# Three rotating score banks, maxima by halves, and nine-column turning products in a two-layer decoder kernel

## The reference, cut to what matters

```
h  = layernorm(x);  x = x + Wo . attention(q, k, v of h, 16 heads of 8, causal, q and k normalised per head) + bo
h  = layernorm(x);  x = x + Wproj . attention(h; ctx, 16 heads of 8, window |i-j| <= 64) + bproj
h  = layernorm(x);  x = x + mxfp4_quantised(h) . mxfp4_quantised(W) + bias
attention = softmax over the keys of (q.k + mask), times v
```

## Time and profile before

| what | us |
|---|---|
| median of three runs | 1455.29 |
| the profiled execution | 1459.37 |
| its span | 1457.6 |
| span from the first maximum of the third phase to the end | 516.3 |
| PE busy in it, DVE, ACT, POOL | 452.04, 354.21, 317.53, 320.32 |

### The profile page before, as it was taken

How to read it: one execution, slowest core, us unless ns; L and a number is a source line. 1 busy time by engine, 2 the same in 40 slices (tenths; PEclk the granted TensorE clock), 3 DMA queues, 4 the chain that set the end, 5 groups by cost and what they waited for, 6 DMA issues and landing times.

```text
span 1457.6 us, 42538 instructions
## 1 busy us (share of the span) xinstructions
PE 1294.8 (89%) x15257; PEld 942.1 (65%) x15257; DVE 1081.9 (74%) x2573; ACT 1049.3 (72%) x2841; POOL 633.9 (43%) x844
## 2 busy tenths in 40 slices
PE   4358999999999999999984999889889989999995
PEld 1125676666666666767674999856656666676664
DVE  6998889999899988876665344466668778686665
ACT  2128999999999999999981566647666766766653
POOL 0012424353444434310215554448675776655663
PEclk9999999999999999999995999979999999999997
DMA  6942242413214241020112332220101010000000
GB/s 145 242 121 57 52 102 53 113 49 95 66 48 100 52 108 49 16 94 2 52 35 66 101 96 75 96 84 22 32 10 42 11 41 11 26 25 4 25 11 16
DMA packets 83579, 89.00 MB, mean 61 GB/s; under 512 B 15792, under 2 KB 72752, under 8 KB 78768
## 3 DMA queue, kind: packets, MB, share of 16 engines
q1 hardware_dynamic: 77424, 77.10, 20.3%
q0 software_dynamic: 4096, 8.40, 2.0%
q10 hardware_dynamic: 1856, 0.79, 0.2%
HBM read 64.76 MB, written 17.83 MB: 57 GB/s over the span
## 4 chain that ended last, share of the span: by engine, by line
PE 60%; DVE 13%; ACT 10%; issue 8%; POOL 5%; DMA 2%; ACTq 0%; another core or an unknown queue 0%; DVEq 0%; SPq 0%; POOLq 0%
PE P L796 7%; PE P L958 7%; PE P L2114 5%; PE P L1579 4%; PE P L1612 4%; PE P L814 3%; PE P L940 3%; ACT pr L1019 3%; PE P L917 3%; PE P L928 3%; PE P L912 3%; PE P L2176 2%; PE P L2132 2%; PE P L835 2%; PE P L2069 2%
## 5 line engine op out<-in xcount | busy, mean ns | idle before, releaser
L2433 DVE TENSOR_REDUCE mx<-P 128x8 f32<-128x1024 f32 x128 | 156.5, 1223 | 123.8 <-PE P L2114 85.3
L1019 ACT ACTIVATE pr<-P,nm 128x256 f32<-128x256 f32 x512 | 238.6, 499 | 5.9 <-DVE nm L1217 5.7
L2326 ACT ACTIVATE et<-P 128x1024 f32<-128x1024 f32 x128 | 131.0, 1024 | 122.6 <-PE P L2121 110.2
L1217 DVE TENSOR_REDUCE nm<-P 128x4 f32<-128x1024 f32 x128 | 156.1, 1219 | 25.9 <-PE P L796 23.5
L796 PE MATMUL P<-kt_w,qt 64*128 64x256 f32 x1024 | 145.2, 402 | 4.6 <-ACT pr L1019 4.6
L1001 ACT COPY ptS<-P 128x512 f32<-128x512 f32 x256 | 138.1, 598 | 8.7 <-PE P L814 8.4
L992 ACT ACTIVATE pr<-pr,ri 128x256 f32<-128x256 f32 x254 | 119.6, 536 | 24.6 <-DVE pr L1190 24.0
L704 POOL TENSOR_TENSOR kv_qk<-kv_qk,mixing 128x512 f32<-128x512 f32 x48 | 61.0, 1271 | 151.9 <-DVE pr L1190 151.9
L1675 ACT ACTIVATE hT<-P,mixing 128x128 f32<-128x128 f32 x284 | 81.0, 368 | 61.1 <-PE P L1579 56.8
L698 POOL TENSOR_TENSOR kv_qk<-kv_qk,r_w 128x512 f32<-128x512 f32 x48 | 61.0, 1270 | 145.6 <-DVE pr L1190 100.0
L1019 ACT ACTIVATION_READ_ACCUMULATOR pr<-P,nm 128x1 f32 x512 | 118.2, 231 | 0.0
(11 more groups left out here) (351 smaller groups left out, 3652.4 us busy)
## 6 DMA issues: line engine op xcount, KB each, us to landing
kv_qk<-scr_v SPq DMA_DIRECT2D x16, 1024.0 KB, 8.0
r_w<-scr_r SPq DMA_DIRECT2D x16, 1024.0 KB, 10.8
xt<-scr_xs SPq DMA_DIRECT2D x71, 64.0 KB, 1.8
scr_ys<-yt SPq DMA_DIRECT2D x71, 64.0 KB
x<-in_x SPq DMA_DIRECT2D x8, 256.0 KB, 10.2
scr_v<-mixing SPq DMA_DIRECT2D x8, 256.0 KB, 2.5
scr_r<-mixing SPq DMA_DIRECT2D x8, 256.0 KB, 2.0
xb<-in_x SPq DMA_DIRECT2D x8, 256.0 KB, 3.3
```

The lines of the kernel that those rows point to most:

```text
L1019: e = nc.scalar.activation(pr[:, s % 3, h * KEYS:(h + 1) * KEYS], scores(s)[:, h // 2, (h % 2) * KEYS:(h % 2 + 1) * KEYS], ACT.Exp, bias=n ...
L1217: nc.vector.tensor_reduce(nm[:, s % 3, 0:4].rearrange("p (a h) -> p a h", a=2), scores(s).rearrange("p a (h k) -> p a h k", k=KEYS), AX.X, ...
L2326: nc.scalar.activation(et[:, u % 4, :, :, :], scoresT, ACT.Exp).then_inc(S["h_exp"], 1)
L2433: nc.vector.tensor_reduce(mx[:, n % 2, 8 * r:8 * r + 8].rearrange("p (k a) -> p k a", k=2), scores, AX.X, ALU.max, negate=True).then_inc(S ...
```

## The change

1. **Score banks.** Unit `s` puts its two halves of scores into banks `SCORE_BANKS[(2s+k) % 3]` of 0, 1 and 6. The mask of half `h` waits for the maximum of half `h-3` only. Each maximum is taken by halves, two instructions of 512 columns.
2. **Turning back** is done by two ordinary products with `ot` as weights and 36 columns of the identity (nine of each head's 32) instead of two transposes of 128 columns. The result has 144 columns and lies in bank 4 beside the output product.
3. **The output product** moves ahead of the turning back in PE's order, and its addition on DVE from the end of the slot to right behind the division.
4. **Projections** to q and k go in pairs (`qk0`, `qk1`: two products of 256 columns, one copy of 512 by ACT) through bank 7; their slots and some in `MIDDLE` change.
5. **The maxima** are turned between the masks and the scores of the next even slot, not at the odd slot's end.

```diff
-        "dxt": -25, "bias": -25, "qk0": -24, "qk1": -23, "qk2": -22, "qk3": -21, "square": -21, "v": -19, "reduce": -20,
+        "dxt": -25, "bias": -25, "qk0": -23, "qk1": -21, "square": -21, "v": -19, "reduce": -20,
...
-        "dxt": 11, "bias": 11, "qk0": 12, "qk1": 13, "qk2": 14, "qk3": 15, "square": 15, "v": 13, "reduce": 16,
+        "dxt": 11, "bias": 11, "qk0": 13, "qk1": 15, "square": 15, "v": 17, "reduce": 16,
...
-MIDDLE = (("qt0", 1), ("kt3", 1), ("qt3", 1), ("kt1", 2), ("kt2", 2), ("qt0", 3), ("kt1", 3), ("kt3", 3), ("qt2", 3),
+MIDDLE = (("qk0", 1), ("kt3", 2), *[(_name, _g) for _name in ("kt2", "qt1") for _g in range(4, GROUPS - 1)], ("qt0", 1), ("kt3", 1), ("qt3", 1), ("kt1", 2), ("kt2", 2), ("qt0", 3), ("kt1", 3), ("kt3", 3), ("qt2", 3),
...
+            SCORE_BANKS = (0, 1, 6)
-            qk_bank = P[:, 4, 2 * T:4 * T]
-            turned = P[:, 6, :]
+            turned = P[:, 4, T:T + H * (DH + 1)]
+            def score_bank(s, k):
+                return P[:, SCORE_BANKS[(2 * s + k) % 3], :]
+            def half(s, k):
+                return 2 * s + k + 1
...
+                def products(s, middle):
+                    for k in range(2):
+                        g = self_at(s, f"qk{k}")
+                        if g and ((f"qk{k}", g) in MIDDLE) == middle:
+                            bank7_free(f"qk{k}", g)
+                            pe.wait_ge(S["h7_read"], filled("dxt", g))
+                            for i in range(2):
+                                b = 2 * k + i
+                                m = nc.tensor.matmul(bank7[:, 256 * i:256 * i + 256], xTd[:, b * T:(b + 1) * T], wD[:, 0:256],
+                                                     start=True, stop=True)
+                            m.then_inc(S["h7"], 1)
...
-                        if s:
-                            pe.wait_ge(S["h_max"], s)
+                        if s == 0:
...
                         for k in range(2):
-                            nc.tensor.matmul(P[:, k, :], identb[:, :], bcast(maskb[:, local, :], 1, 4),
+                            if half(s, k) == 3:
+                                pe.wait_ge(S["m_y"], TILES)
+                            if half(s, k) > 3:
+                                pe.wait_ge(S["h_max"], half(s, k) - 3)
+                            nc.tensor.matmul(score_bank(s, k), identb[:, :], bcast(maskb[:, local, :], 1, 4),
                                              start=True, stop=False)
...
+                    if s % 2 == 0:
+                        maxima(s // 2 - 1)
                     for a in range(4):
...
-                        if qk_before[s + 1]:
-                            pe.wait_ge(S["qk_read"], qk_before[s + 1])
...
-                            m = nc.tensor.transpose(turned.rearrange("p (t a r x) -> p t r a x", t=2, a=2, r=2)[:, t, u % 2],
-                                                    ot[:, u % 2, t, :], ident[:, :])
+                            m = nc.tensor.matmul(turned.rearrange("p (t a r j x) -> p t r a j x", t=2, a=2, r=2, j=2)[:, t, u % 2],
+                                                 ot[:, u % 2, t, :],
+                                                 ident[:, :].rearrange("p (a j x) -> p a j x", a=2, j=2)[:, :, :, 0:DH + 1],
+                                                 start=True, stop=True)
...
-                    if s % 2:
-                        maxima(s // 2)
...
-                        nc.vector.tensor_reduce(mx[:, n % 2, 8 * r:8 * r + 8].rearrange("p (k a) -> p k a", k=2), scores,
-                                                AX.X, ALU.max, negate=True).then_inc(S["h_max"], 1)
+                        for k in range(2):
+                            nc.vector.tensor_reduce(mx[:, n % 2, 8 * r + 4 * k:8 * r + 4 * k + 4],
+                                                    score_bank(s, k).rearrange("p (a n) -> p a n", a=4),
+                                                    AX.X, ALU.max, negate=True).then_inc(S["h_max"], 1)
```

More of the change, by code:

```diff
@@ L2113, in score @@
                         cols, part = slice(b * T, (b + 1) * T), slice(64 * r + 32 * k, 64 * r + 32 * k + 32)
-                        return nc.tensor.matmul(scores[:, k, a, :], q[part, a, cols], keys[part, a, cols], start=False,
+                        return nc.tensor.matmul(score_bank(u, k)[:, a * T:(a + 1) * T], q[part, a, cols], keys[part, a, cols], start=False,
                                                 stop=(a == 3))
@@ L2155, in tensor_program @@
                                 m.then_inc(S["h_st"], 1)
+                    products(s, True)
                     operands(s, True)
@@ L2179, in tensor_program @@
                         m.then_inc(S["h_pv"], 1)
[L2182 to L2191, removed]
+                    u = s - 8
+                    if 0 <= u < UNITS_H and u % 2:
+                        n = pass_of(u)
+                        pe.wait_ge(S["h_oth"], n + 1)
+                        if n:
+                            pe.wait_ge(S["h_add"], n)
+                        if u + 1 < UNITS_H:
+                            pe.wait_ge(S["h_on"], n + 1)
+                        nc.tensor.matmul(wo_bank, oTh[:, n % 2, :], (wE if unit(u)[0] else wDo)[:, :], start=True,
+                                         stop=True).then_inc(S["h_wo"], 1)
                     u = s - 6
@@ L2214, in tensor_program @@
                         nc.tensor.transpose(oT_bank, on3[:, n % 2, :], ident[:, :]).then_inc(S["h_tr"], 1)
[L2215 to L2218, removed]
-                        if qk_before[s + 1]:
-                            pe.wait_ge(S["qk_read"], qk_before[s + 1])
[L2221 to L2235, removed]
+                    products(s, False)
                     g = self_at(s, "v")
@@ L2300, in operands, with products @@
                                                  scale=gbs[:, 6:7]).then_inc(S["h7_read"], 1)
+                def products(s, middle):
+                    for k in range(2):
+                        g = self_at(s, f"qk{k}")
+                        if g and ((f"qk{k}", g) in MIDDLE) == middle:
+                            got(f"qk{k}", g)
+                            if k == 0:
+                                act.wait_ge(S["d_qkn"], 2 * (g - 1))
+                            nc.scalar.copy(qkv[:, g % 2, 2 * k:2 * k + 2, :].rearrange("p b n -> p (b n)"), bank7)\
+                              .then_inc(S["h7_read"], 1)
                 for s in range(FIRST_H, LAST_H):
@@ L2344, in scalar_program @@
                           .then_inc(S["h_ot"], 1)
[L2346 to L2352, removed]
-                    turned_rows(s, False)
[L2355 to L2360, removed]
-                          .then_inc(S["p_qp_read"], 1)
+                    turned_rows(s, False)
+                    products(s, False)
                     g = self_at(s, "v")
@@ L2446, in vector_program @@
                                                 bcast(ri3[:, :], 2, DH), ALU.mult).then_inc(S["h_on"], 1)
+                    u = s - 8
+                    if 0 <= u < UNITS_H and u % 2:
+                        local, g, b, r = unit(u)
+                        n = pass_of(u)
+                        dve.wait_ge(S["h_wo"], n + 1)
+                        if local:
+                            dve.wait_ge(S["e_xb"], GS * g + b + 1)
+                        else:
+                            dve.wait_ge(S["d_xb"], g + 1)
+                        nc.vector.tensor_tensor(home(g)[:, b, :], home(g)[:, b, :], wo_bank, ALU.add)\
+                          .then_inc(S["h_add"], 1)
+                        dve.wait_ge(S["h_add"], n + 1)
                     g = self_at(s, "reduce")
```

48 lines of the change are left out of this document (13 added, 35 removed), and 4 rows, old and new, of tables (SELF, SELF_BY_SLOT).

## The result

The changed kernel takes 1462.04 us (median of 7 runs, 1459.03 to 1463.13) where the kernel before takes 1455.29 (7 runs): a ratio of 1.0041, interval 1.0029 to 1.0053. It is slower by 0.4%, where 1450 us, a gain, had been forecast. It is the outcome and the size of rival 1.

A forecast was written before the change was run, and what follows sets the result against it. PE was taken as the bound, busy 452 of 516 us in the third phase, with the scores-maximum-masks loop setting light slots. Terms -20 - 5 + 21 - 1 = -5 us gave about 1450 us, range 1437 to 1465 (8 in 10).

The forecast's parts named there:

- rival 1: Weight loads win: full slots pay 0.20 us, waits give 12, projections 3, turning back costs 25; 1465 us, chance 0.25.
- I take -20 us: PE's waits at masks and maxima product, 18.8 us listed: most go by rotation and moved maxima; ends -12 and -28.
- light slots shorter by 0.3 and full ones longer by 0.13: Third-phase slots: without bank-7 work 2.8 and 3.05 us, with four transposes 3.2 and 3.45.
- Together -5 us: Output product's wait for ACT's projection copy goes, projections pair: -6, +1.5, +1.6, -2; ends 0 and -9.
- +0.20 us a unit: Turning back on PE: four weight loads, 0.47 us against 0.27 until the next product; +25.6 us over 128 units.
- 4 us of cover: Part of the turning back's +25.6 us hidden where PE waits for POOL or late ACT, leaving +21 us.
- +10 to +29: Ends given for the turning back's net cost, taken as +21 us.
- The rest, -1: DVE's earlier addition, output product's wait for `on`, later maxima to ACT, earlier first masks: -1 us in all.
- point of decision: rival 1 decides once less than about 16 us of waits are recovered at a price of 21.
- Rival 4: Short products are cheap: turning back free or a gain of some 0.1 us a unit; 1416 us, chance 0.03.
- Rival 3: Longer slots give ACT, POOL, DVE time; PE's POOL waits shrink, cover 12 rather than 4; 1440 us, chance 0.16.

The follow-up runs named there:

- e9: The kernel before with the maxima moved and taken by halves, each mask waiting for its own bank's half, projections one by one; 1447.56 us.
- e4: The kernel before with paired projections, maxima moved and by halves, two score banks, old transposes, output product and addition as before; 1449.05 us.
- e5: The changed kernel with two score banks in place of three, each mask waiting for its own bank's last half; 1462.78 us.
- e7: The changed kernel with the turning back issued twice a unit, writing the same values; 1505.25 us.
- e10: The kernel before with the maxima by halves alone, the maxima product staying at the odd slot's end; 1450.22 us.
- e3: The kernel before with only the maxima moved, between masks and scores of the next even slot; 1454.22 us.
- e1: The kernel before with the nine-column turning back alone, in bank 6 as before; 1466.15 us.
- e2: The kernel before with only the projections in pairs through bank 7, with their tables; 1456.27 us.
- e8: The changed kernel with the output product behind the turning back, DVE's division waiting for it as well; 1463.89 us.
- e12: e11 with DVE's addition also moved right behind the division; 1448.12 us.
- e11: e4 with three steps of ACT (normalisation and quantisation) a slot later in groups 0, 1 and 5; 1447.91 us.

## Why the prediction was wrong

Mean lengths of the slots from the 8th to the 126th, from mask to mask, in us, by what stands in them; each number is a sum over the group divided by its count. "In the middle" are slots with such work in the kernel before (11) or in the changed one (7 more); the 17th and 29th, light before, hold the projection to values in the changed kernel and count among the projections:

| slots | count | before | e9 | e4 | e5 | after | e7 |
|---|---|---|---|---|---|---|---|
| no bank-7 work | 16 | 3.39 | 2.99 | 3.05 | 3.00 | 2.94 | 3.35 |
| four transposes at the end | 35 | 3.43 | 3.37 | 3.42 | 3.54 | 3.61 | 3.93 |
| the turned rows of the local attention at the end | 22 | 3.37 | 3.62 | 3.55 | 3.72 | 3.71 | 4.07 |
| projections, values, turned rows for them, quantised product | 26 | 3.96 | 3.85 | 3.60 | 3.74 | 3.71 | 4.12 |
| bank-7 work in the middle | 18 | 4.40 | 4.36 | 4.48 | 4.51 | 4.50 | 4.70 |
| the 34th and 35th | 2 | 6.73 | 5.81 | 6.89 | 6.63 | 6.85 | 6.97 |
| sum of all | 119 | 443.9 | 435.6 | 434.5 | 445.3 | 446.3 | 486.4 |

(The sum of before is that of its profiled execution, 4 us over the median.)

- **"I take -20 us" for the waits: this step failed.** Halves and moved maxima together are -8 (e9), alone -5 (e10) and -2 (e3), and beside the new turning back the third bank adds nothing (e5). The prediction had most of the waits go. In e9 many of them only moved: PE's products still wait 8.1 us at the masks and 0.4 for `ot` of the 18.8, and the weight loads at the masks wait as long as they had at both places. What brought the list down to 3.7 in the changed kernel is in good part the longer turning back (e1: 7.4, with a slower kernel), and a wait that ends because PE comes later is no time won.
- **The forecast itself had the contradiction:** light slots shorter by 0.3 and full ones longer by 0.13, but there are 16 light slots in both kernels, and 57 with transposes at the end. 16 x 0.3 is a gain of 4.8 us, 57 x 0.13 a loss of 7.4. The other 46 slots would have had to give 8 us for the forecast of -5; they gave 4. The light slots won 0.45, more than forecast, and the full ones lost 0.24, nearly twice as much: they had no wait to give, as rival 1 has it. The saving in a light slot is also partly given back in the next: in e9 and e4 a light slot falls to 2.70 us and the even one behind it rises from 3.07 to 3.39 (the 96th), as its second mask's weight load then waits 0.38 us for DVE's maximum, which the moved product stands behind.
- **"Together -5 us" for projection pairs and the output product's wait: wrong too.** It is 0 (e2), and the pairs add nothing in e4 against e9. The wait before the output product disappeared from the list, and the pair's own slot became longer by 0.3 us.
- **"+0.20 us a unit": right; "4 us of cover": far too low.** By the starts of the products (medians) the block from the last product with the values to the product behind the turning back, the output product and the turned heads takes 0.81 us in even slots where it took 0.59, and 0.89 in odd ones where it took 0.70: +0.23 and +0.19, 27 us in all, where 25.6 had been forecast. The passes cost the 0.111 us of the earlier trace rows (e7). The Trainium skill ("TensorE: Matmul & The Clock Gate", section "LDWEIGHTS (loading the stationary operand)") has a load of 128 columns take an estimated 107 ns whatever its rows; the trace, with 0.111 to 0.112 us a pass, agrees. In the odd slots the output product's second pass now starts 0.21 us after its first (0.11 before), but one of the four passes behind it starts 0.03 us after the one before it, so that the sum is as forecast. With the output product behind the turning back (e1, e8) the odd block takes 0.97 us, +0.27. So some 27 us of work came. 14 of them arrived in the time (e5 against e4), and the other 13 went under waits; in e1, with waits still there to cover it, 32 came and 10 arrived. By the table (e4 to e5) the light slots and those with middle work took almost nothing of it (3.05 to 3.00, 4.48 to 4.51), and the 36th takes 4.87 us with either turning back (before, e1). That in the middle ones ACT's copies set the length is argued, not shown. The net of +14 is within my +10 to +29.
- **"The rest, -1":** nothing that could be measured, by e8 and e12.
- **The sum:** -8 + 0 + 14 = +6, and +6.7 was measured. The forecast was -20 - 5 + 21 - 1 = -5. Both errors in the waits went one way (17 us), and the cover made up for 7. That the total missed by no more than 11 us is luck to that extent.
- **Rival 1** had -12, -3 and +25: right in the sign and in its reason, that full slots have no wait to give, and within 3 us in the time. The nearness is partly luck: it had 7 us too much won by the waits and projections and 11 too much lost by the turning back, with too little cover. Its point of decision, less than 16 us recovered at a price of 21, was met: 8 were recovered, at a price of 14. Rival 4 is out by e7. Rival 3 had the net cost of the turning back (14 us) right, but not its PE waits for POOL, which went from 6.5 to 7.0.
- **Open:** where the kernel before's profiled execution spent its 4 us over the median. Single slots differ between kernels without a part of the change to explain it. The 61st took 5.39 us before, 6.72 after and 6.9 in e8, but 4.5 in e5; PE stands idle in it for 1.99 us before and 2.12 after, ended by nothing that the profile shows. So the 34th, 35th and 61st are no evidence for either side. What the third bank would give beside the transposes is open too: the waits at the masks that e9 still lists are the ones it is made for.

## What to carry to other kernels

Before a list of waits is summed as a gain, multiply the slot lengths that you forecast by how many slots there are of each kind: where most slots are full on the busiest engine, work added to that engine counts in each, and a wait removed counts only in the few that had it. Then look, in a run that has that part alone, whether the wait has gone, has moved to the next instruction, or has merely been covered by work that was added. Here an fp32 product of 8 or of 36 columns cost two passes of 0.111 us, each with its weight load, and two such products in place of two transposes cost 0.2 us, so on this engine the trade of a transpose for a narrow fp32 product was a bad one. Try the parts of a change one by one: here two (halves and moved maxima) win 0.6% together, three (the third bank, the pairs, and the places of the output product and its addition) do nothing that can be measured, and one, the turning back, loses about 1%, more than the others win.

## What the runs showed of the hardware that was not expected

- The second pass of the output product, fp32 with 128 columns, starts 0.112 us after its first behind the transposes (before), but 0.213 behind products of another tile shape (32 rows, changed kernel) and 0.192 behind the passes of 36 columns (e1, e8), where the shape does not change. A product of 36 columns behind those of the other shape has its second pass 0.132 us after its first. These are medians; why they differ no run here tells.
- A long stall of PE cost more than its length here. In e4 PE did nothing for 4.1 us up to 1078.94, and TensorE was granted half its clock (1.2 GHz in place of 2.4) from 1076.9 to 1083.7 us; in e11, where the stall of 3.85 us ends at 1089.60, from 1088.3 to 1095.1. The four passes of the projections took 1.91 us in that stretch of e4 (at 1080.65) and 1.03 a slot before (at 1071.46). The kernel before and the changed one have the same stretch, both from 1082.1 to 1088.9, at the end of stalls of 3.23 and 3.42 us (to 1082.72 and 1082.43), so it does not explain their difference. In the changed kernel's 61st slot the clock is half from 1191.4 to 1194.8, behind the idle 2.12 us, and in the kernel before it stays full there, behind 1.99. Windows of these stretches, of e4 and then of e11, the clock in the column behind POOL:

```profile
1076.90:1083.70 6.80, 4.76 (x29) 3.02 (x33) 1.33 (x4) 3.17 (x7) 4.59 (x7) 0.50 0.04 11
```

```profile
1088.30:1095.10 6.80, 5.50 (x56) 3.60 (x57) 5.86 (x11) 1.92 (x3) 1.09 (x2) 0.50 0.00 0
```

- Two DVE instructions of the stalled stretch in e11 took 2.64 and 2.68 us, where the same lines have medians of 0.344 and 1.09 us; POOL was at work through nearly all of both, from 1080.98 to 1085.74; what held them no run here tells.
